# Post-LN attention and mixture of experts on one core: the causal mask of the score tile is added by VectorE instead of by a matrix product

## The reference, cut to what matters

```
latent_kv = x @ w_kv_down
kv = latent_kv @ w_kv_up
q = (x @ w_q).reshape(Bx, Tx, N_HEAD, HEAD_SIZE)
att = jnp.einsum('bqhd,bkhd->bhqk', q, k) * scale
causal = jnp.tril(jnp.ones((Tx, Tx), dtype=bool))
att = jnp.where(causal, att, -jnp.inf)
att = jax.nn.softmax(att, axis=-1)
y = jnp.einsum('bhqk,bkhd->bqhd', att, v)
...
x = _layernorm(x + _L0_attn_ref(...), axis=-1)
x = _layernorm(x + _L0_ffn_ref(...), axis=-1)
```

## Time and profile before

| | |
|---|---|
| time, median of 3 runs | 3475.12 us (3470.42 to 3476.35) |
| profiled execution, its own time | 3469.43 us |
| its span | 3467.5 us |
| PE busy | 3185.9 us, 92% of the span |
| DVE busy | 2097.3 us, 60% |
| ACT busy | 1840.7 us, 53% |
| POOL busy | 1388.5 us, 40% |
| granted TensorE clock, mean | 0.963 of full speed |

### The profile page before, as it was taken

The page is one execution under the profiler, slowest core; times in us unless marked ns, Lnnn a source line. Parts: engine busy times, 40 slices in busy tenths (PEclk is TensorE's granted clock), DMA queues, the critical chain, the costliest instruction groups (busy, mean ns, idle before and its releaser), DMA issues. The chain is left out here.

```text
span 3467.5 us, 69523 instructions
## 1 busy us (share of the span) xinstructions
PE 3185.9 (92%) x21406; PEld 2506.0 (72%) x21406; DVE 2097.3 (60%) x4881; ACT 1840.7 (53%) x4007; POOL 1388.5 (40%) x1512
## 2 busy tenths in 40 slices
PE   5999999999999999999999999979908999999991
PEld 3767676667667676767676776679908999999991
DVE  1666566666666666666666666657584555455546
ACT  2667566666666666666666666633203343343430
POOL 0434343333334343334333333312214656565543
PEclk7999999999999999999999999989959999999996
DMA  6444444444445444444444444267402333333226
GB/s 204 106 114 108 99 113 104 102 102 119 104 100 123 101 107 110 108 98 114 107 99 117 106 111 101 65 250 268 180 27 64 72 68 74 67 76 68 41 42 202
DMA packets 184386, 376.26 MB, mean 109 GB/s; under 512 B 23872, under 2 KB 108224, under 8 KB 181952
## 3 DMA queue, kind: packets, MB, share of 16 engines
q1 hardware_dynamic: 144704, 308.52, 34.6%
q0 software_dynamic: 29696, 50.48, 7.3%
q10 hardware_dynamic: 9600, 12.58, 1.0%
HBM read 123.97 MB, written 79.76 MB: 59 GB/s over the span
## 5 line engine op out<-in xcount | busy, mean ns | idle before, releaser
L243 POOL TENSOR_SCALAR prob<-prob,inv 128x128 f32<-128x128 f32 (+7 forms) x1024 | 774.9, 757 | 1311.5 <-DVE inv L589 1311.5
L584 DVE TENSOR_REDUCE neg_max<-s_ps 128x1 f32<-128x128 f32 (+7 forms) x1024 | 773.2, 755 | 725.6 <-PE s_ps L370 709.9
L495 ACT ACTIVATE prob<-s_ps,neg_max 128x128 f32<-128x128 f32 (+7 forms) x1024 | 758.0, 741 | 199.6 <-DVE neg_max L584 182.4
L380 PE MATMUL t_ps<-ident,prob 128*128 128x128 f32 x4608 | 683.5, 275 | 9.1 <-ACT prob_t L573 2.5
L368 PE MATMUL s_ps<-k_hh,q_hl 128*128 128x512 f32 (+3 forms) x1536 | 591.6, 385 | 44.6 <-ACT prob L495 26.6
L573 ACT ACTIVATE prob_t<-t_ps 128x512 f32<-128x512 f32 (+3 forms) x768 | 415.8, 541 | 396.9 <-PE t_ps L380 396.2
L396 PE MATMUL o_ps<-prob_t,v 128*64 128x512 f32 (+3 forms) x3072 | 537.5, 492 | 1.5 <-DVE y L606 1.5
L369 PE MATMUL s_ps<-k_lz,q_hl 128*128 128x512 f32 (+3 forms) x1536 | 513.2, 346 | 0.0
L380 PEld LDWEIGHTS t_ps<-ident,prob 128*128 128x128 f32 x4608 | 495.7, 141 | 19.6 <-ACT prob_t L573 14.1
L368 PEld LDWEIGHTS s_ps<-k_hh,q_hl 128*128 128x128 f32 x1536 | 290.9, 189 | 176.4 <-issue 92.0
L396 PEld LDWEIGHTS o_ps<-prob_t,v 128*64 128x64 f32 x3072 | 203.8, 136 | 278.0 <-issue 251.6
(11 more groups left out here) (152 smaller groups left out, 5502.7 us busy)
## 6 DMA issues: line engine op xcount, KB each, us to landing
k_hh<-k_high SPq DMA_DIRECT2D x256, 256.0 KB, 4.6
q_hl<-q_high SPq DMA_DIRECT2D x128, 256.0 KB, 4.0
q_hl<-q_low SPq DMA_DIRECT2D x128, 256.0 KB, 4.2
k_lz<-k_low SPq DMA_DIRECT2D x128, 256.0 KB, 5.4
y_d<-y SPq DMA_DIRECT2D x128, 256.0 KB, 3.8
c_yt<-y_d SPq DMA_DIRECT2D x16, 2048.0 KB, 8.5
w_raw<-w SPq DMA_DIRECT2D x16, 1024.0 KB, 7.5
a_xt<-x_t SPq DMA_DIRECT2D x8, 1024.0 KB, 7.6
```

Source lines behind the costliest of these rows:

```text
L243: pool.tensor_scalar(pr, pr, inv[:, s % 4:s % 4 + 1], 1.0, ALU.mult, ALU.mult).then_inc(norm_done, 1)
L380: mm = pe.transpose(t_ps[k % 2][:, j * P:(j + 1) * P], prob[s % 4][:, (first + j) * P:(first + j + 1) * P], ident[:])
L495: act.activation(prob[s % 4][:, 0:(q + 1) * P], s_ps[s % 2][:, 0:(q + 1) * P], ACT.Exp, bias=neg_max[:, s % 4:s % 4 + 1], accum_out=total[ ...
L584: dve.tensor_reduce(neg_max[:, s % 4:s % 4 + 1], s_ps[s % 2][:, 0:(q + 1) * P], AX.X, ALU.max, negate=True).then_inc(max_done, 1)
```

## The change

The bf16 pair `ident_b` and `mask_b` goes, and with it the product of line 370. A mask of 128 by 128 in fp32 (`mask`) takes its place in SBUF. `scores_done` is now posted by the last `k_lz` product. In `maximum`, a VectorE addition of `mask` to the diagonal 128 columns, in place in PSUM, comes ahead of the reduction, and the reduction waits for it by a new semaphore, `masked`.

```diff
@@ constants, on POOL
-            pool.tensor_copy(ident_b[:], ident[:]).then_inc(const_ready, 1)
-            pool.memset(mask_b[:], 0.0).then_inc(const_ready, 1)
-            pool.wait_ge(const_ready, 4)
-
-            pool.affine_select(out=mask_b[:], in_=mask_b[:], compare_op=ALU.is_ge, fill=MASKED, base=0,
+            pool.memset(mask[:], 0.0).then_inc(const_ready, 1)
+            pool.wait_ge(const_ready, 3)
+
+            pool.affine_select(out=mask[:], in_=mask[:], compare_op=ALU.is_ge, fill=MASKED, base=0,
                                pattern=[[-1, P]], channel_multiplier=1).then_inc(const_ready, 1)
@@ scores, on PE
                     pe.matmul(out, q_hl[u][h][:, cols], k_hh[u][h][:, w], start=True, stop=False)
-                    pe.matmul(out, q_hl[u][h][:, cols], k_lz[u][h][:, w], start=False, stop=True)
-                mm = pe.matmul(s_ps[s % 2][:, q * P:width], ident_b[:], mask_b[:], start=False, stop=True,
-                               skip_group_check=True)
+                    mm = pe.matmul(out, q_hl[u][h][:, cols], k_lz[u][h][:, w], start=False, stop=True)
                 mm.then_inc(scores_done, 1)
@@ maximum, on DVE
                 dve.wait_ge(scores_done, 16 * n + s + 1)
+                diagonal = s_ps[s % 2][:, q * P:(q + 1) * P]
+                dve.tensor_tensor(diagonal, diagonal, mask[:], ALU.add).then_inc(masked, 1)
+                dve.wait_ge(masked, 16 * n + s + 1)
                 dve.tensor_reduce(neg_max[:, s % 4:s % 4 + 1], s_ps[s % 2][:, 0:(q + 1) * P], AX.X, ALU.max,
                                   negate=True).then_inc(max_done, 1)
```

More of the change, by code:

```diff
@@ L116, in attention_stage @@
         ident = sb("ident", [P, P])
-        ident_b = sb("ident_b", [P, P], BF16)
-        mask_b = sb("mask_b", [P, P], BF16)
+        mask = sb("mask", [P, P])
         xt = sb("b_xt", [P, KC, T])
@@ L155, in attention_stage @@
         w_in = [sem(f"b_w_in{u}") for u in range(2)]
-        scores_done, max_done, exp_done, inv_done, norm_done = (
-            sem(n) for n in ("scores_done", "max_done", "exp_done", "inv_done", "norm_done"))
+        scores_done, masked, max_done, exp_done, inv_done, norm_done = (
+            sem(n) for n in ("scores_done", "masked", "max_done", "exp_done", "inv_done", "norm_done"))
         turned = sem("turned")
@@ L338, in _ @@
             load_weights(1, 1)
-            sp.wait_ge(const_ready, 9)
+            sp.wait_ge(const_ready, 8)
             place_queries(0, 0)
@@ L443, in first @@
             def first():
-                pe.wait_ge(const_ready, 9)
+                pe.wait_ge(const_ready, 8)
                 for c in range(2):
```

## The result

| | before | after |
|---|---|---|
| median us | 3473.91 (3470.42 to 3476.35) | 3571.15 (3568.44 to 3574.89) |
| span of the profiled execution | 3467.5 | 3566.6 |
| PE busy | 3185.9 | 3202.5 |
| DVE busy | 2097.3 | 2391.2 |
| from the first scores of the last pair's last step to the end | 1222.5 | 1222.8 |

The change makes the kernel slower: 1.0282 times the time before, 95% interval 1.0269 to 1.0295, or +97 us. The forecast was 3530 with a range to 3562. The direction came out, and so did the mechanism in an ordinary pair; the size did not.

The account below looks back on a forecast made before the run. PE was taken as the bound nearly everywhere, the scores, maximum, `exp` loop right behind. +0.90 us a pair over 63 pairs, +57 on 3469.4, makes 3526; 5.7 for the median makes 3532, stated as 3530, range 3484 to 3562.

Parts of the forecast that it names:

- I count 63 pairs: Attention: +0.90 us a pair times 63 pairs of heads, one left for start and end, makes +57 us.
- The term of an ordinary pair, +0.90: Lateness carried through one pair of heads: 6 D - 1.02 us, +0.90 with D = 0.32.
- D: How much later each DVE reduction starts for the addition and its wait: 0.32 us, bounds 0.21 and 0.44.
- the 1.02: Us a pair taken off six D in the carried sum, for slacks, saved PE products and earlier `scores_done`.
- All sixteen products saved are in the 1.02: Claim that the pair's sum already counts every mask product PE saves, 0.067 us each.
- The addition at 0.29 and the wait of 0.03: On DVE before each reduction: addition 0.29 us, then 0.03 us until the reduction starts; together 0.32.
- The places: Points in the pair's wide steps, on DVE and PE, with lateness forecast from D - 0.15 to 5 D - 0.58.
- PE keeps its gain: Rival: additions hide in DVE's idle time, PE saves 69 us, kernel takes 3406 us; chance 10%.
- gain and loss cancel: Rival: two or three of the six places in a pair have slack, 3468 to 3482 us; chance 8%.
- The wait is free: Rival: the reduction's wait for DVE's addition costs nothing, D = 0.21, 3490 us; chance 10%.
- A dearer addition: Rival: DVE's PSUM addition and wait cost more, D from 0.37 to 0.44, 3550 to 3577 us; chance 14%.
- The signs: Expected after-profile: `exp` waits over 80 us, PE busy less 227.5, pairs about 34.5 us, wide-step DVE over 90%.

Follow-up runs that it names:

- after_pad8: Changed kernel with eight semaphore increments ahead of DVE's loop, shifting its code: 3546.08 us, 1.0213.
- both: Kernel before, mask product kept, plus a same-size DVE addition into a spare SBUF tile that each reduction waits for: 3606.07 us, 1.0381.
- no_mask: Changed kernel without its DVE addition, so the causal mask is left out altogether: 3423.82 us, 0.9862.
- both_free: As `both`, but the addition writes to four spare tiles in turn and nothing waits for it: 3551.08 us, 1.0221.
- the later split: Weights' split moved one slot later (`W_SPLIT` 5 instead of 4) in either kernel: changed kernel 3551.73 us, kernel before 3462.15 us.
- covered: Changed kernel with DVE masking only steps 0 to 4, 6, 7, 8, 12 and 13, PE the other six: 3474.66 us, 1.0006.
- after_pads: Changed kernel with eight semaphore increments on DVE and 64 on PE ahead of the loop: 3558.69 us, 1.0244.
- after_w5: Changed kernel with the weights' split one slot later (`W_SPLIT` 5 instead of 4): 3551.73 us, 1.0229.

## Why the prediction was wrong in size

- *The range failed at "I count 63 pairs".* It took one ordinary pair for all. At six of them the loop branches back, and there the changed kernel stands a second time: 24 us of the +97, shown by `after_pad8`, which without it takes 3546, inside the range. Six stands of 3.2 us are 19 of the 24; the clock below may be the rest. The row for 600 to 1200 us averages over these pairs. A view of the branch before would have shown the first stand (2.46 us) and that such pairs are unlike the others, but not the second, which that kernel does not have. This is the largest part of the miss and not all of it: the next item adds 11 us, and the sixth, seventh, second and third pairs together some 3.
- *The term of an ordinary pair, +0.90, measured +1.08.* D was 0.333 for 0.32, which makes 6 x 0.013 = 0.08 of the difference. The other 0.10 is in the 1.02, of which 0.37 is slack and 0.65 is products and the earlier signal. `both`, where PE saves nothing, leaves 6 x 0.325 - 1.60 = 0.35 for slack. So products and signal gave back 2.00 - 0.35 - 1.08 = 0.57 for the 0.65. Together 0.18 x 63 = 11 us. "All sixteen products saved are in the 1.02" is not what the steps of the sum say: they count eight on PE's path and take two of them back at step 7.
- *The addition at 0.29 and the wait of 0.03* held: 0.299 and 0.034.
- *The places:* each of the seven lies within 0.14 us. The error enters between the scores of steps 13 and 14 on PE (0.69 and 0.75 late, by the terms 0.68 and 0.61); why PE does not gain its product there is open.
- *PE keeps its gain* (3406): the gain is real, 49 us in `no_mask`, and the additions cost more. Refuted, as is *gain and loss cancel*.
- *The wait is free* (3490): refuted by `both` against `both_free`, 0.77 a pair. *A dearer addition* (3550 to 3577) holds the time but not the cause: its D began at 0.37. Its remark that DVE splits `xt` and `lat` in eight pairs a batch is wrong; that is the seventh pair of each batch but the last.
- *The signs:* the wait for `exp` went from 47 to 112 us (over 80 forecast), the transposes of slot 14 wait 0.54, the stages after the attention did not move, and DVE in the wide steps is at 89%, just short of the 90 forecast. A pair of 34.56 answers to the "about 34.5". One sign was wrong: PE's busy time does not fall by the mask group's 227.5 us but rises by 16.6. `no_mask` shows 65.9 less for the same products taken out; the group's time overlaps its neighbours'. That the rest is products which stand longer while they wait is argued, not shown.

Open is why the later split shortens the changed kernel's branch pair (to 40.48) and hardly that of the kernel before (to 36.57). Open too is the seventh pair, 0.6 us or more over an ordinary one in every version, up to 2.3 in `covered`; it is the pair in whose slots DVE and ACT also split the next `xt` and `lat`, and no run took that work away. That a stand is the arrival of instructions rests on shifting code, on the "issue" rows and on the instruction queues' packets; no row names what DVE waits for.

## What to carry to other kernels

Work taken off the busiest engine gains only where the loop behind it has room: carry the lateness step by step through the tightest stretch, and move only the steps that end ahead of a wait (here ten of sixteen). Count the unlike iterations apart, above all the one at a loop's branch, before multiplying by the number of iterations. And when a kernel's time moves by a per cent more than its ordinary iteration says, look for "issue" waits on an engine that has work, and shift its code by a few instructions before you put the whole difference down to the change.

## What the runs showed of the hardware

- At the loop's branch DVE stands for 2.1 to 2.5 us (2.18 in the changed kernel, 2.46 in the one before), which I put down to its code. In some versions a second stand of about 3 us comes an instruction or two later. Eight instructions that do nothing, ahead of the loop, took the changed kernel from 3571 to 3546 us; eleven took the kernel before from 3473 to 3484.
- Semaphore increments by themselves start 0.093 us apart on DVE (`after_pad8`) and 0.15 us apart on PE (`after_pads`, 64 of them in 9.8 us).
- The clock follows the stand. In the changed kernel PE is busy for 3.74 us of the 9 around the branch. In the 8 us behind them its granted clock is 0.79 of full: the mean of a part at the lower level (1.2 GHz) and the rest at the higher (2.4 GHz).

```profile
663.00:672.00 9.00, 3.74 (x26) 3.31 (x26) 3.63 (x9) 1.96 (x4) 0.93 (x2) 1.00 0.91 203
672.00:680.00 8.00, 7.54 (x38) 6.38 (x38) 5.21 (x13) 5.82 (x12) 2.69 (x3) 0.79 0.02 9
```

  At the same branch the kernel before, where PE is busy for 3.96 of 5 us, keeps the higher level:

```profile
641.00:646.00 5.00, 3.96 (x28) 3.34 (x28) 2.54 (x6) 2.25 (x4) 1.12 (x2) 1.00 1.01 223
646.00:655.00 9.00, 8.61 (x61) 7.38 (x61) 6.04 (x14) 8.50 (x18) 4.75 (x6) 1.00 0.37 88
```

  By the clock's records that kernel keeps the higher level at three of its six branches, with pairs of 36.26 us, and is at the lower one for 3.4 us at each of the other three, with pairs of 37.07. From 100 to 2200 us it spends 10 us at the lower level, the changed kernel, where every branch has some of it, 34 us, and `after_w5` 27. At 0.81 us for each 3.4 us, the 24 us more at the lower level cost some 6 us, an estimate from these two kinds of pair.

- DVE's addition of 128 columns, read from PSUM and written back there, takes 296 ns, where the one instruction in SBUF alone took 292.
